# Graph network on one core: counts copied by ScalarE into a bf16 ring, four count tables fetched earlier, first eight K/V gathers issued one stage earlier

## The chip, the cores and the metric

The kernel runs on one core of one Trainium2 chip. The metric is the device time of one execution in microseconds (us), as the median of the runs. A core has TensorE (PE, matrix products, with a separate weight load PEld), VectorE (DVE), ScalarE (ACT), GpSimd (POOL) and SyncE (SP, which here only issues DMAs and waits). Each engine works through its own instructions in order; semaphores are all that ties them together. SBUF is the on-chip memory of 128 partitions, PSUM the accumulator memory that PE writes.

## What is computed

A graph has 3125 nodes with 96 features each and 103125 directed edges (50000 random pairs in both directions and one loop per node), sorted by destination. Four layers follow one another, each added to its input and layer-normalised:

```python
edge_index = jnp.stack([src, dst])
x = _layernorm(x + _L0_gnn_ref(x, L0_gnn_weight, L0_gnn_bias, src, dst))
x = _layernorm(x + _L1_gnn_ref(x, edge_index, edge_weight, W1, b1, W2, b2, W3, b3))
x = _layernorm(x + _L2_gnn_ref(x, edge_index, W1, b1, W2, b2, gn...))
x = _layernorm(x + _L3_gnn_ref(x, edge_index, edge_attr_96, Wq, bq, Wk, bk, We, be, Wv, bv))
# L0: agg = segment_sum(feat[src] * out_deg[src]**-0.5, dst) * in_deg**-0.5; agg @ W + b
# L1: three times  segment_sum((x @ W)[src] * norm, dst) + b,  norm from weighted degrees
# L2: twice        graph_norm(segment_sum((x @ W)[src], dst) + b), relu, + identity
# L3: score = exp(clip(sum(K[src] * Q[dst] * E) / sqrt(12), -5, 5)) for 8 heads;
#     segment_sum(V[src] * score, dst) / (segment_sum(score, dst) + 1e-6)
```

## The kernel before

The first three layers don't gather. They multiply by dense 3125x3125 tables: `w_blocks` (f32) holds the sum of edge weights from node s to node d, `c_blocks` (bf16) the number of such edges. Both lie in HBM as NT=25 blocks of 125 destination columns (LANES). The stages, in order:

- `examine_edges` (0 to 17 us) loads indices, checks them, and prepares per-edge numbers.
- `add_edges` (to 571 us) builds the tables. Edges lie in columns of 128. A batch g is G=8 columns (101 batches), a four q is Q4=4 columns (202 fours), a round r is four batches and moves on by about one block. For a batch DVE makes one-hot vectors: `hot_lo` (which source lane, L761), `hot_hi` (L772), `third` (L778, one part of the split edge weight), `middle` (L783, another part, for columns BY_ACT=4 to 7), and `hot` (which destination place of a window, L769, once for a four). ACT multiplies `hot_lo` by the parts of the weight (L678, twelve per batch). PE multiplies these into one PSUM bank pair per four, `ps_four[u]`, u = 0 or 1: zero (L717), counts (L723), out-degrees (L724), weights (L729). The result covers a window of REACH=20 destination columns, for 25 source tiles and two tables: 1000 elements per partition. DVE's `add` (L797) adds them to the ring `strip`, f32, [128, 2 tables, 25, 520]: four slots of 125 columns and an overlap of 20, at a column read from `ring_col`. The windows of successive fours overlap or follow on one another.
- In each round, `finish` (L803) closes a block; every fourth round `fold` (L807) adds the overlap back to the ring's beginning. ACT `convert`s the block's counts to bf16 into `counts` in five pieces of 625 elements (L668). SP stores weights (L608) and counts (L610). POOL clears the slot again with memsets (L630, L636): count head after the conversion, weight head and both tails after the store of the weights. DVE waits for `heads_clear` and `tails_clear` at the start of later rounds.
- `graph_layers` (572 to 1354 us): 150 jobs, six passes of 25 blocks. Passes 0, 4 and 5 use count tables (PE L1281), passes 1 to 3 weight tables (L1269); SP's `load(j)` fetches a job's table into a ring, four slots for counts. One count table, `first_table`, is fetched in `add_edges` already. In pass 0 the stores of the last weight block (five pieces, L1053) stand between the loads, then `wrow` (L1056) is read from HBM, and DVE's `weight_sums` (L1453) sum it in five pieces, one a job, before job 17 (`W_DEG_AT`). The stage ends with projections to K, V, Q, stored by SP to `kv_dram` (L1067) and `q3_dram` (L1072); SP waits until all have landed, and an all-engine barrier follows.
- `attention_windowed` (from 1354.6 us) walks 202 fours through a ring of ten slots: POOL gathers K/V rows (L2350, four indirect DMAs a four, indices copied by ACT L2368), SP loads edge attributes, destinations and Q rows (L2317, L2318, L2320), PE multiplies (L2441, L2443, L2455), DVE makes scores and messages (L2510 to L2530). POOL waits for `msg_ready` of the four that had its slot before.

The order on each engine is the order of the code in its block; there is no scheduler.

## Time and profile before

| | us |
|---|---|
| median of 3 runs | 2692.86 |
| lowest, highest | 2684.45, 2707.22 |
| profiled execution, device time | 2688.49 |
| its span in the profile | 2685.7 |

| engine | busy us | share of the span |
|---|---|---|
| PE | 2006.5 | 75% |
| DVE | 1384.0 | 52% |
| ACT | 1004.8 | 37% |
| POOL | 957.3 | 36% |

The profiled execution's own time is 2.8 us above its span. Shares over the whole span say little, since the stages have different limits. The page's second part divides the span in forty slices of 67 us: in slices 2 to 8 DVE shows 9 of 9 tenths, in the graph layers PE does, and in the attention none does. The rows further down are from views of single stages: windows (busy time per engine in a stretch), groups by line (mean duration of one instruction and what it waited for), waits, and the timeline (start and duration of single instructions; in it an instruction's duration overlaps the next one's by about 0.1 us, so the cost of one is read as the distance between two starts).

### The profile page before, as it was taken

The numbers are of one execution on the slowest core, as the hardware profiler recorded it, in microseconds if no ns is written. First come the engines' busy times: TensorE is split into PE (matmuls) and PEld (weight loads), VectorE is DVE, ScalarE is ACT, GpSimd is POOL, SyncE is SP. The second block draws the span as 40 slices with busy tenths as digits, with TensorE's granted clock in tenths as the row PEclk, the third lists the DMA queues.
The fourth block names the chain that finished last, engine by engine and source line by source line (L and its number), as shares of the span: only waits on it lengthen the run. The fifth ranks groups of instructions, "written<-read, shape, count | busy, mean of one in ns | idle before, by whom it ended". The sixth has DMA issues, their size and how long they took to land. (4 is left out here: it accounts for less than half of the span.)

```text
span 2685.7 us, 50009 instructions
## 1 busy us (share of the span) xinstructions
PE 2006.5 (75%) x14784; PEld 1733.1 (65%) x14785; DVE 1384.0 (52%) x3361; ACT 1004.8 (37%) x2697; POOL 957.3 (36%) x947
## 2 busy tenths in 40 slices
PE   7888888879999999999716565565656656665665
PEld 3666666657999999878515555555555555555565
DVE  6999999976111134332414444444444444444445
ACT  5788888853100011121312332333233233333332
POOL 2122223210000000000255566565655655666662
PEclk9999999989999999999755555555555555555555
DMA  1677787797888777657244444444444444444442
GB/s 49 95 122 109 116 128 117 115 197 245 308 288 292 287 288 281 215 174 243 63 129 135 127 125 125 116 132 122 124 130 121 125 118 128 129 132 124 126 134 56
DMA packets 225304, 415.59 MB, mean 155 GB/s; under 512 B 130819, under 2 KB 150297, under 8 KB 215449
## 3 DMA queue, kind: packets, MB, share of 16 engines
q1 hardware_dynamic: 186414, 334.76, 45.7%
q0 software_dynamic: 38784, 79.48, 11.4%
q8 instruction: 59, 0.97, 0.1%
q14 instruction: 47, 0.38, 0.0%
HBM read 347.71 MB, written 66.43 MB: 154 GB/s over the span
## 5 line engine op out<-in xcount | busy, mean ns | idle before, releaser
L2350 POOL DMA_INDIRECT attention_windowed_vkv<-kv_dram,ttention_windowed_vsrc x808 | 783.9, 970 | 507.9 <-issue 252.7
L2441 PE MATMUL attention_windowed_vps_e<-attention_windowed_vwe,attention_windowed_vattr 97*128 97x96 f32 x1616 | 413.1, 428 | 179.9 <-issue 113.8
L2441 PEld LDWEIGHTS attention_windowed_vps_e<-attention_windowed_vwe,attention_windowed_vattr 97*128 97x128 f32 x1616 | 370.7, 329 | 181.4 <-issue 153.5
L2455 PE MATMUL attention_windowed_vps_s<-attention_windowed_hot,attention_windowed_vmsg 128*104 128x32 f32 x1616 | 324.8, 357 | 212.3 <-issue 100.8
L2455 PEld LDWEIGHTS attention_windowed_vps_s<-attention_windowed_hot,attention_windowed_vmsg 128*104 128x104 f32 x1616 | 302.8, 286 | 253.0 <-issue 199.0
L1269 PE MATMUL graph_layers_acc<-graph_layers_w_tab,graph_layers_g 125*96 125x125 f32 x3750 | 417.7, 269 | 0.0
L1269 PEld LDWEIGHTS graph_layers_acc<-graph_layers_w_tab,graph_layers_g 125*96 125x96 f32 x3750 | 406.6, 163 | 0.0
L678 ACT ACTIVATE add_edges_hot_lo<-add_edges_hot_lo,parts 128x128 bf16<-128x128 bf16 x1212 | 372.6, 393 | 89.5 <-DVE add_edges_hot_lo L761 89.5
L2383 ACT ACTIVATE attention_windowed_vmsg<-ttention_windowed_vscore 128x32 f32<-128x32 f32 x202 | 46.5, 230 | 801.9 <-DVE ttention_windowed_vscore L2516 498.8
L729 PE MATMUL add_edges_ps_four<-add_edges_hot,add_edges_hot_lo 128*128 128x200 bf16 x2424 | 332.1, 258 | 0.0
L1099 POOL CAST graph_layers_g<-graph_layers_w_tab 125x480 bf16<-125x480 f32 x4 | 2.3, 585 | 742.5 <-ACT graph_layers_w_tab L1146 735.8
L797 DVE TENSOR_TENSOR strip<-strip,add_edges_ps_four 128x1000 f32 x202 | 244.1, 1209 | 23.3 <-PE add_edges_ps_four L729 22.5
L630 POOL MEMSET strip<- 128x500 f32 (+1 forms) x92 | 127.2, 1412 | 319.8 <-ACT add_edges_counts L668 220.9
L2443 PE MATMUL attention_windowed_vps_q<-ttention_windowed_q_rows,attention_windowed_hot_T 96*128 96x96 bf16 x808 | 119.3, 276 | 155.4 <-issue 153.0
L2530 DVE TENSOR_TENSOR ttention_windowed_sums_T<-ttention_windowed_sums_T,attention_windowed_vps_s 104x32 f32 x202 | 38.2, 189 | 365.6 <-remote 259.1
L723 PE MATMUL add_edges_ps_four<-add_edges_hot,add_edges_hot_lo 128*128 128x200 bf16 x808 | 211.8, 262 | 0.0
L2510 DVE TENSOR_TENSOR attention_windowed_vprod<-attention_windowed_vkv,attention_windowed_vps_q 128x384 f32<-128x384 f32 x202 | 110.8, 549 | 195.5 <-remote 151.1
L2443 PEld LDWEIGHTS attention_windowed_vps_q<-ttention_windowed_q_rows,attention_windowed_hot_T 96*128 96x128 bf16 x808 | 101.1, 153 | 167.1 <-issue 165.5
L1281 PE MATMUL graph_layers_acc<-graph_layers_g,graph_layers_c_tab 125*128 125x288 bf16 (+1 forms) x1400 | 196.8, 290 | 3.0 <-DMA graph_layers_c_tab<-c_blocks 2.4
L729 PEld LDWEIGHTS add_edges_ps_four<-add_edges_hot,add_edges_hot_lo 128*128 128x128 bf16 x2424 | 178.0, 99 | 1.1
L1432 DVE SCALAR_TENSOR_TENSOR graph_layers_z<-graph_layers_prod,graph_layers_dis,graph_layers_b 125x96 f32<-125x96 f32 x75 | 23.9, 318 | 298.3 <-PE graph_layers_prod L1249 298.3
L717 PE MATMUL add_edges_ps_four<-add_edges_noughts,add_edges_nought 1*128 1x500 bf16 x404 | 121.4, 380 | 64.1 <-DVE strip L797 63.7
(245 smaller groups left out, 2666.5 us busy)
## 6 DMA issues: line engine op xcount, KB each, us to landing
graph_layers_w_tab<-w_blocks SPq DMA_DIRECT2D x75, 1562.5 KB
graph_layers_c_tab<-c_blocks SPq DMA_DIRECT2D x56, 800.0 KB
attention_windowed_vattr<-in_attr_T SPq DMA_DIRECT2D x202, 192.0 KB
attention_windowed_vdrow<-dstf_dram SPq DMA_DIRECT2D x202, 192.0 KB
w_blocks<-strip SPq DMA_DIRECT2D x24, 1562.5 KB, 14.6
c_blocks<-add_edges_counts SPq DMA_DIRECT2D x24, 800.0 KB, 5.8
first_table<-c_blocks SPq DMA_DIRECT2D x19, 800.0 KB, 4.4
attention_windowed_vkv<-kv_dram,ttention_windowed_vsrc POOLq DMA_INDIRECT x808
```

Of the source, the lines that this page charges most:

```text
L630: nc.gpsimd.memset(strip[:, table, :, slot(b)][:, :, columns], 0.0).then_inc(done, 1)
L678: done = nc.scalar.activation(hot_lo[s][:, 1 + part, j, :], hot_lo[s][:, 0, j, :], ACT.Copy, scale=parts[:, part, bass.ds(g * G + j, 1)])
L717: nc.tensor.matmul(both[:, table, 0:NT * REACH], nought[:], noughts[:], start=True, stop=False)
L723: nc.tensor.matmul(cells[:, 0], hot_lo[s][:, 0, e, :], hot[s][:, e, :], start=False, stop=m == Q4 - 1)
L729: last = nc.tensor.matmul(cells[:, 1], hot_lo[s][:, 1 + part, e, :], hot[s][:, e, :], start=False, stop=m == Q4 - 1 and part == 2)
L797: nc.vector.tensor_tensor(cells, cells, ps_four[u][:, :, 0:NT * REACH].rearrange("p c (t n) -> p c t n", n=REACH), ALU.add).then_inc(added, 1)
L1269: return nc.tensor.matmul(acc[j % 2][0:D, 0:L], g[(k - 1) % 2][0:L, t, :], w_tab[s][0:L, t, :], start=t == 0, stop=t == NT - 1)
L1281: return nc.tensor.matmul(acc[j % 2][:, 0:width], c_tab[s][0:L, t, :], g3[0:L, t, 0:width], start=t == 0, stop=t == NT - 1)
L2350: nc.gpsimd.indirect_dma_start(out=kv[s][:, k, :], out_offset=None, in_=kv_dram, in_offset=bass.IndirectOffsetOnAxis(ap=src4[s][:, k:k + 1 ...
L2441: nc.tensor.matmul(ps_e[s % BANKS][:, k, :], attr[:, s, k * P:(k + 1) * P], wes[:], start=True, stop=True)
L2443: last = nc.tensor.matmul(ps_q[s % BANKS][:, k, :], hot_T[s][:, k, :], q_rows[:, s, :], start=True, stop=True)
L2455: last = nc.tensor.matmul(ps_s[s % 2], msg[s][:, k, :], hot[s][:, k, :], start=k == 0, stop=k == Q4 - 1)
```

## The change

Three edits, of which the first is the largest.

**Counts.** The ring `strip` now holds weights alone (f32, 500 elements per window), and counts have a ring of their own, `count_ring`, in bf16. A four's first column can hold counts of the four before, so DVE adds that one column (25 elements); the nineteen behind it are new, and ACT copies them out of PSUM (`copy_counts`, 475 elements, over what was there). DVE's `add` becomes an add of 25 and one of 500 elements. ACT's `convert` goes; BY_ACT falls from 4 to 3, so ACT has eleven multiplications a batch, and DVE's `middle` covers five columns (640 elements) for four. POOL converts the whole block with one copy (3125 elements per partition), folds the counts' overlap (`fold_counts`), and clears half as many elements. PE waits for `copied` and `middle_done` too; DVE and ACT wait for POOL's `ring_free`.

**Tables.** Four count tables (FIRST_TABLES) are fetched during blocks 17 to 20 of `add_edges`, and `graph_layers` starts without loads 1 to 3. The last weight block is stored in one DMA ahead of `load(4)`; `wrow` is read after `load(6)`. `weight_sums` has eight pieces and stands where DVE waits for ACT's standard deviation; `W_DEG_AT` is 18. `y5` has three buffers.

**Gathers.** POOL copies the indices of two fours (AHEAD=2) and issues their eight gathers at the end of `graph_layers`, as soon as K/V are stored. SP there waits for the Q stores only. In the attention ACT and POOL begin with four 2; SP's wait for `ones_ready` moved to PE. `examine_edges` checks in addition that no window begins 20 or more columns behind the one before (four small DVE instructions).

```diff
-                if b == NT - 3:
-                    sp.wait_ge(counts_stored, 16)
-                    sp.dma_start(first_table[:].rearrange("p t c -> p (t c)"), c_blocks[0]).then_inc(first_landed, 16)
+                q = b - (NT - 8)
+                if 0 <= q < FIRST_TABLES:
+                    sp.wait_ge(counts_stored, 16 * (q + 1))
+                    sp.dma_start(first_tables[q][:].rearrange("p t c -> p (t c)"), c_blocks[q]).then_inc(first_landed[q], 16)
...
-                clear(b, 0, head, heads_clear)
-                pool.wait_ge(weights_stored[b % SLOTS_B], 16 * (b // SLOTS_B + 1))
-                clear(b, 1, head, heads_clear)
-                clear(b, 0, tail, tails_clear)
-                clear(b, 1, tail, tails_clear)
...
+            def fold_counts(b):
+
+                pool.wait_ge(added, groups_of(b))
+                pool.wait_ge(copied, groups_of(b))
+                nc.gpsimd.tensor_tensor(count_ring[:, :, 0:REACH], count_ring[:, :, 0:REACH], count_ring[:, :, RING:RING + REACH],
+                                        ALU.add).then_inc(count_folded, 1)
+                pool.wait_ge(count_folded, b // SLOTS_B + 1)
...
+                pool.wait_ge(added, groups_of(b))
+                pool.wait_ge(copied, groups_of(b))
+                if b > 0:
+                    pool.wait_ge(counts_stored, 16 * b)
+                nc.gpsimd.tensor_copy(counts[:, :, 0:LANES], count_ring[:, :, slot(b)]).then_inc(converted, 1)
+                if first:
+                    pool.wait_ge(converted, b + 1)
+                    nc.gpsimd.memset(count_ring[:, :, 0:REACH], 0.0)
+                pool.sem_inc(ring_free, 1)
...
-                done = nc.scalar.activation(counts[:, some, 0:LANES], strip[:, 0, some, bass.ds((r + 2) % SLOTS_B * LANES, LANES)], ACT.Copy)
...
+            def copy_counts(q, at):
+
+                act.wait_ge(columns_added, q + 1)
+                cells = ps_four[at[1]][:, 0, 0:NT * REACH].rearrange("p (t n) -> p t n", n=REACH)[:, :, 1:REACH]
+                nc.scalar.activation(count_ring[:, :, 1:RING + REACH][:, :, bass.ds(at[0], REACH - 1)], cells, ACT.Copy).then_inc(copied, 1)
...
+                        if later_batch and j == 2:
+                            copy_counts(2 * g - 2, (at[0], 0))
+                        if later_batch and j == 6:
+                            copy_counts(2 * g - 1, (at[1], 1))
+                        if j == 1 and k == batches[0] and reaches(r, 3):
+                            act.wait_ge(ring_free, r - 2)
...
                             pe.wait_ge(added, q - 1)
+                            pe.wait_ge(copied, q - 1)
...
+                            if e == BY_ACT:
+                                pe.wait_ge(middle_done, g + 1)
...
-                nc.vector.tensor_tensor(cells, cells, ps_four[u][:, :, 0:NT * REACH].rearrange("p c (t n) -> p c t n", n=REACH),
-                                        ALU.add).then_inc(added, 1)
+                if reaches(q, 1):
+                    dve.wait_ge(copied, q)
+                first = count_ring[:, :, bass.ds(at, 1)]
+                nc.vector.tensor_tensor(first, first, new[:, 0, :, 0:1], ALU.add).then_inc(columns_added, 1)
+                nc.vector.tensor_tensor(cells, cells, new[:, 1], ALU.add).then_inc(added, 1)
...
                 if reaches(r, 3):
-                    dve.wait_ge(heads_clear, 2 * (r - 2))
+                    dve.wait_ge(ring_free, r - 2)
+                    dve.wait_ge(heads_clear, r - 2)
                     dve.wait_ge(overlap_clear, (r - 3) // SLOTS_B + 1)
                 if reaches(r, 4):
-                    dve.wait_ge(tails_clear, 2 * (r - 3))
+                    dve.wait_ge(tails_clear, r - 3)
...
-            load(1)
...
-            load(2)
-            load(3)
...
+            sp.dma_start(w_blocks[NT - 1].rearrange("p (t c) -> p t c", c=L), strip[:, :, 0:L]).then_inc(last_stored, 16)
+            load(4)
+            load(5)
...
-            for j in range(4, 4 + 5):
-                load(j)
-                some = chunk(j - 4)
-                sp.dma_start(w_blocks[NT - 1].rearrange("p (t c) -> p t c", c=L)[:, some, :], last_weights[:, some, :]).then_inc(last_stored, 16)
-            load(9)
-            sp.wait_ge(last_stored, 16 * 6)
+            load(6)
+            sp.wait_ge(last_stored, 16 * 2)
             sp.dma_start(wrow[:], w_blocks[:, L + 1, :].rearrange("b (t c) -> b t c", c=L)).then_inc(wrow_loaded, 16)
...
-            sp.wait_ge(tables_stored, 16 * (2 + 2 * CHUNKS))
+                sp.dma_start(q3_dram[area, :].rearrange("(t p) c -> p t c", p=L), g3[0:L, chunk(c), 0:D3]).then_inc(q3_stored, 16)
+            sp.wait_ge(q3_stored, 16 * (1 + CHUNKS))
+            pool.wait_ge(early_src_ready, AHEAD)
+            pool.wait_ge(kv_stored, 16 * (1 + CHUNKS))
+            for q in range(AHEAD):
+                for k in range(Q4):
+                    nc.gpsimd.indirect_dma_start(
+                        out=early_kv[q][:, k, :], out_offset=None, in_=kv_dram,
+                        in_offset=bass.IndirectOffsetOnAxis(ap=early_src[q][:, k:k + 1], axis=0)).then_inc(early_landed[q], 16)
...
+                if j < NT and 0 <= j - (W_DEG_AT - 2 - W_SUM_PARTS) < W_SUM_PARTS:
+                    weight_sums(j - (W_DEG_AT - 2 - W_SUM_PARTS))
                 dve.wait_ge(sd_ready, n + 1)
...
-            for s in range(SLOTS):
+            for s in range(AHEAD, SLOTS):
                 gather(0, s)
```

What stands in a row on DVE in `add_edges`, from a batch's first one-hot to its `middle`, before (after it come the second `hot` and the second four's add):

```order
L761 TENSOR_TENSOR add_edges_hot_lo<-add_edges_lane_of,add_edges_lo 128x8x126
L772 TENSOR_TENSOR add_edges_hot_hi<-add_edges_tile_of,add_edges_hi 128x208
L778 TENSOR_TENSOR add_edges_hot_lo<-add_edges_hot_lo,add_edges_third 128x1024
L769 TENSOR_TENSOR add_edges_hot<-add_edges_place_of,add_edges_place 128x800
L797 ISA
L797 TENSOR_TENSOR strip<-strip,add_edges_ps_four 128x50x20
L783 TENSOR_TENSOR add_edges_hot_lo<-add_edges_hot_lo,add_edges_middle 128x512
```

and after; an ISA row ahead of an add sets its address:

```order
L809 TENSOR_TENSOR add_edges_hot_lo<-add_edges_lane_of,add_edges_lo 128x8x126
L820 TENSOR_TENSOR add_edges_hot_hi<-add_edges_tile_of,add_edges_hi 128x208
L826 TENSOR_TENSOR add_edges_hot_lo<-add_edges_hot_lo,add_edges_third 128x1024
L817 TENSOR_TENSOR add_edges_hot<-add_edges_place_of,add_edges_place 128x800
L849 ISA
L849 TENSOR_TENSOR count_ring<-count_ring,add_edges_ps_four 128x25
L850 ISA
L850 TENSOR_TENSOR strip<-strip,add_edges_ps_four 128x25x20
L831 TENSOR_TENSOR add_edges_hot_lo<-add_edges_hot_lo,add_edges_middle 128x640
```

Each 1000-element add has become one of 25 and one of 500, and `middle` (L783, now L831) has grown.

ACT in a batch of `add_edges`, after the change; `parts` are the multiplications, L703 is the first of the copies of counts (L701 and the ISA row set its address):

```order
L714 ACTIVATE add_edges_hot_lo<-add_edges_hot_lo,parts 128x128
L714 ISA
L714 ACTIVATE add_edges_hot_lo<-add_edges_hot_lo,parts 128x128
L701 REGISTER_ALU
L703 ISA
L703 ACTIVATE count_ring<-add_edges_ps_four 128x25x19
L714 ISA
L714 ACTIVATE add_edges_hot_lo<-add_edges_hot_lo,parts 128x128
```

Two such copies stand among the multiplications of a batch, after the 6th and the 10th of the eleven. Before, two copies of 625 elements from `strip` to `counts` stood in most batches.

POOL for the first blocks, before (`x2`: twice in a row):

```order
L636 MEMSET strip 128x50x20
L630 MEMSET strip 128x25x20 x2
L630 MEMSET strip 128x25x105 x2
L630 MEMSET strip 128x25x20 x2
L630 MEMSET strip 128x25x105 x2
```

and after, for a block that folds and the next:

```order
L648 TENSOR_TENSOR count_ring<-count_ring 128x25x20
L656 MEMSET count_ring 128x25x20
L662 COPY add_edges_counts<-count_ring 128x25x125
L665 MEMSET count_ring 128x25x20
L670 MEMSET strip 128x25x20
L672 MEMSET strip 128x25x20
L673 MEMSET strip 128x25x105
L662 COPY add_edges_counts<-count_ring 128x25x125
L672 MEMSET strip 128x25x20
L673 MEMSET strip 128x25x105
```

Of POOL's operations before, all in this stretch write only; now one copy a block, and a two-input add every fourth, read SBUF.

## Rows read from the trace of the kernel before

**Rows 1.** windows; columns: stretch, length, busy us (count) per engine, PE clock, DMA

```profile
150.00:250.00 100.00, 87.25 (x858) 62.76 (x857) 99.87 (x162) 83.38 (x255) 29.17 (x22) 1.00 0.73 112
```

**Rows 2.** timeline, DVE, one batch; start us, duration us, line, operation

```profile
281.51 0.70 DVE L761 TENSOR_TENSOR add_edges_hot_lo<-add_edges_lane_of,add_edges_lo 128x1008 bf16<-128x1008 bf16 x1
...
282.99 0.59 DVE L769 TENSOR_TENSOR add_edges_hot<-add_edges_place_of,add_edges_place 128x800 bf16<-128x800 bf16 x1
283.48 1.21 DVE L797 TENSOR_TENSOR strip<-strip,add_edges_ps_four 128x1000 f32 x1
284.58 0.44 DVE L783 TENSOR_TENSOR add_edges_hot_lo<-add_edges_hot_lo,add_edges_middle 128x512 bf16<-128x512 bf16 x1
284.92 0.59 DVE L769 TENSOR_TENSOR add_edges_hot<-add_edges_place_of,add_edges_place 128x800 bf16<-128x800 bf16 x1
...
286.51 0.70 DVE L761 TENSOR_TENSOR add_edges_hot_lo<-add_edges_lane_of,add_edges_lo 128x1008 bf16<-128x1008 bf16 x1
```

**Rows 3.** groups, 100 to 550 us, DVE; count, busy us, mean ns

```profile
L797 DVE TENSOR_TENSOR strip<-strip,add_edges_ps_four 128x1000 f32 x176 | 212.9, 1210 | 0.8 <-PE add_edges_ps_four L729 0.2
```

**Rows 4.** waits, 100 to 550 us; total us, times, longest us

```profile
PE add_edges_ps_four L717 <- DVE strip L797: 56.8, 87, 1.4
...
DVE strip L797 <- PE add_edges_ps_four L729: 0.2, 1, 0.2
```

**Rows 5.** groups, 100 to 550 us, ACT

```profile
L678 ACT ACTIVATE add_edges_hot_lo<-add_edges_hot_lo,parts 128x128 bf16<-128x128 bf16 x1054 | 324.5, 393 | 55.6 <-DVE add_edges_hot_lo L761 55.6
L668 ACT ACTIVATE add_edges_counts<-strip 128x625 bf16 x110 | 79.0, 718 | 11.5 <-DVE strip L803 11.5
```

**Rows 6.** timeline, ACT, a copy out of PSUM

```profile
1304.46 0.57 ACT L1151 COPY graph_layers_w_tab<-graph_layers_acc 96x500 f32<-96x500 f32 x1 [1.36 <-PE graph_layers_prod L1329]
```

**Rows 7.** groups, 100 to 550 us, POOL

```profile
L630 POOL MEMSET strip<- 128x2625 f32 x44 | 99.8, 2297 | 0.0
L630 POOL MEMSET strip<- 128x500 f32 x44 | 23.3, 529 | 305.5 <-ACT add_edges_counts L668 213.2 <-DMA w_blocks<-strip 92.3
```

**Rows 8.** timeline, POOL, its only conversion of 128 partitions

```profile
569.26 0.99 POOL L644 CAST add_edges_hot_lo<-strip 128x625 bf16<-128x625 f32 x1 [14.57 <-DVE strip L803]
```

**Rows 9.** timeline, POOL, two operations that read SBUF

```profile
1311.94 1.07 POOL L1101 TENSOR_TENSOR graph_layers_rest<-graph_layers_w_tab,graph_layers_g 125x480 f32<-125x480 f32 x1
1313.07 0.59 POOL L1103 CAST graph_layers_g<-graph_layers_rest 125x480 bf16<-125x480 f32 x1
```

**Rows 10.** timeline, DVE, at the same moment

```profile
1311.88 0.16 DVE L1522 TENSOR_TENSOR graph_layers_var<-graph_layers_st 125x5 f32<-125x5 f32 x1
1312.11 0.92 DVE L1524 TENSOR_TENSOR graph_layers_dif<-graph_layers_dif 125x5 f32<-125x5 f32 x1
```

**Rows 11.** page, DMA issues: count, KB each, us from issue to landing

```profile
w_blocks<-strip SPq DMA_DIRECT2D x24, 1562.5 KB, 14.6
```

**Rows 12.** windows of pass 0, with and without weight sums; columns as rows 1

```profile
624.90:652.00 27.10, 24.83 (x196) 18.90 (x195) 20.20 (x74) 7.19 (x28) 0.00 (x0) 1.00 0.61 207
652.00:678.10 26.10, 25.39 (x207) 20.26 (x206) 16.00 (x78) 13.01 (x50) 0.00 (x0) 1.00 0.79 299
```

**Rows 13.** timeline, PE, the stall in pass 0

```profile
620.45 2.34 PE L1281 MATMUL graph_layers_acc<-graph_layers_g,graph_layers_c_tab 125*128 125x289 bf16 x12 [2.35 <-DMA graph_layers_c_tab<-c_blocks]
```

**Rows 14.** timeline, DVE, one weight sum

```profile
632.03 1.31 DVE L1453 TENSOR_REDUCE graph_layers_wsum<-graph_layers_wrow 25x25 f32<-25x625 f32 x1
```

**Rows 15.** timeline, end of graph_layers and start of attention

```profile
1340.82 0.87 SPq L1067 DMA_DIRECT2D kv_dram<-graph_layers_w_tab  x1
...
1355.80 1.16 POOL L2350 DMA_INDIRECT attention_windowed_vkv<-kv_dram,ttention_windowed_vsrc  x1 [0.99 <-ACT ttention_windowed_vsrc L2368]
1357.27 0.96 POOL L2350 DMA_INDIRECT attention_windowed_vkv<-kv_dram,ttention_windowed_vsrc  x1 [0.30 <-issue]
...
1359.18 0.33 SPq L2317 DMA_DIRECT2D attention_windowed_vattr<-in_attr_T  x1
```

**Rows 16.** timeline, POOL, its first wait in attention

```profile
1416.09 0.95 POOL L2350 DMA_INDIRECT attention_windowed_vkv<-kv_dram,ttention_windowed_vsrc  x1 [9.76 <-DVE attention_windowed_vmsg L2520]
```

210 lines of the change are left out of this document (123 added, 87 removed).

## Prediction

> **What bounds the kernel now.** I read the windows of the stages first. From 50 to 568 us `add_edges` runs, and in a window of 100 us DVE is busy 99.87, PE 87, ACT 83, POOL 29 [rows 1]: DVE sets that stage's pace. The waits confirm it: DVE's add waited for PE once in 450 us, for 0.2 us, while PE waited for DVE's adds 56.8 us in all [rows 4]. So PE would need about (450 - 56.8) / 88 batches = 4.47 us a batch where DVE needs 5.00, the distance between two `hot_lo` starts [rows 2]. In the graph layers PE sets the pace; the rows show where it does not: a stall of 2.35 us for a count table [rows 13], and a window with weight sums in which 196 matmuls of the count product took 27.1 us where the next window did 206 in 26.1 [rows 12]. In the attention no engine is full; its first POOL wait for a free slot comes at 1406 to 1416 us [rows 16].
>
> **Part 1, DVE in add_edges.** An add of 1000 elements costs 1.10 us from start to start [rows 2] (176 of the 202 stand in one group with this mean duration, [rows 3]). One of 500 costs 0.55 if all of it scales, about 0.58 with a fixed part; one of 25 about 0.1, since even a five-element operation shows 0.16 with its overlap [rows 10]. Saved: 1.10 - 0.68 = 0.42 an add, 0.84 a batch. `middle` grows by 128 elements: 800 elements cost 0.49 and 512 cost 0.34 [rows 2], so +0.07. Net 0.77 a batch, times 101 batches = -78 us; six folds at half size, -3 us.
>
> Whether the others can follow: ACT made twelve multiplications and 1.25 conversions a batch; now eleven at 0.29 (393 ns less the overlap of 0.10, [rows 5]) = 3.2, and two copies out of PSUM at 0.46 (a 500-element one took 0.57 with overlap, [rows 6]) = 0.9, so 4.1 of DVE's new 5.00 - 0.77 = 4.23. PE needs the 4.47 above, more than 4.23: at most, since a little of it is the wait for ACT. Without another cost, a round of four batches would therefore be PE's 17.9 us, and not DVE's 17.2.
>
> **Part 2, POOL now reads SBUF.** Its memsets before only write. The 3125-element copy of a block does not appear in this trace. Bounds: a memset's slope, (2297 - 529) / 2125 = 0.83 ns an element [rows 7], gives 2.7 us; a conversion of 480 elements took 0.59 us [rows 9], 1.22 ns an element, 3.8 us, or 3.2 if 0.11 of it is fixed as in the memsets; the one conversion on 128 partitions took 0.99 us for 625, beside two casts of DVE [rows 8], 4.9 us. I take 2.9, nearest to the slope and the conversion with its fixed part taken off, because the new copy reads 2-byte elements in rows of 125.
>
> POOL has the time for it (29 of 100 us busy). What matters is DVE: at 1311.94 POOL ran a two-input operation of 1.07 us, to 1313.01; a DVE operation of two SBUF inputs on five elements, started 1312.11, took 0.92 us and ended at 1313.03, where the same kind took 0.16 just before, at a moment with no such POOL operation beside it [rows 9, 10]. So a POOL operation that reads SBUF holds up a DVE operation with two SBUF inputs until it ends. Nearly all of DVE's work in a batch is that; only the adds, which take one input from PSUM, probably run beside it. (The Trainium skill, "SBUF — State Buffer", section "Who interferes with whom", says the same: two SBUF inputs on DVE contend with a GpSimd operation that reads SBUF, not with one that only writes, and the other engine blocks fully. The trace agrees, 0.92 us against 0.16. By that rule this change trades DVE work for DVE standstill.) I count 2.5 us a copy, since POOL most likely gets in beside an add of 0.6 us half of the time or more: 24 copies x 2.5 = +60 us. `fold_counts` (500 elements, two inputs, 1.07 for 480, [rows 9]) seven times, less an overlap: +5. PE and ACT catch up during the standstill: a lag of 4 x (4.47 - 4.23) = 1.0 us a round fits into 2.5.
>
> (The Trainium skill, "GPSIMD Engine Reference", section 3, has a read-bound body at 1.03 cycles an element: 3125 x 1.03 / 1.2 GHz = 2.7 us, an estimate from that page alone; with it the sum would be 5 us lower. The memset slope gives the same.)
>
> Accumulation: -78 - 3 + 60 + 5 = -16 us. The round goes from 4 x 5.00 + 0.5 = 20.5 to about 19.8. The store of the weights (14.6 us, [rows 11]) and the 0.53 us memset behind it still end about 3.5 us ahead of the next use. Copy at 2.7 gives -21; at 3.8 (3.4 net), +5; at 4.9 (4.5 net), +32.
>
> **Part 3, tables and weight sums.** The stall of 2.35 goes, because `wrow` and the five pieces no longer stand between the loads [rows 13]. Behind it PE ran 12 matmuls in 2.34 where it usually takes 1.66: another 1.3 us over that job until the pace returned. Weight sums of 1.31 us [rows 14] sat in DVE's loop: 196 matmuls at the next window's pace are 24.8 us, so 2.3 was lost in 27.1 [rows 12]. Moved to where DVE waits 0.4 to 0.5 us for ACT, in eight pieces of 0.8 us, they still cost some. Together about -6 us; bounds 0 (the large loads collide with the undivided store) and -8. The third `y5` buffer is worth nothing: DVE's and ACT's split of each chunk sets that pace, and POOL was ahead.
>
> **Part 4, early gathers.** The last K/V store is issued at 1340.82 and, with 0.6 MB in 768-byte pieces, I take it as landed at about 1350; attention's first gather starts at 1355.80, the second 1.47 later, and the rest 1.26 apart [rows 15]. Eight early ones from 1350.3 end at 1360.4. POOL holds the barrier about 7 us longer than SP's Q stores did, so attention starts near 1361.5; SP's loads move from 1359.18 to about 1362, but POOL's ninth gather from 1366.1 (1357.27 + 7 x 1.26) to 1362.6. The stage starts later by 2.5 for PE and earlier by 3.5 for POOL. POOL runs on until its slots are full [rows 16], and the DVE fours there are far apart while gathers run; I take -3, between +7 (the barrier's delay carried to the end) and -10. `examine_edges` gets four small DVE operations at 0.15: +0.6.
>
> **Sum.** +0.6 - 16 - 6 - 3 = -24 us. On the profiled execution's 2688.5 that is 2664; its time is 4 us under the median of the runs shown, which spread over 23 us. I say 2665, 1.0% under the median.
>
> **Rivals.**
> - *Copies don't stop DVE* (POOL's read is slow only in itself, or DVE's one-hots pass). Against it: rows 9 and 10. Then PE sets 4.47 x 4 + 0.3 = 18.2 a round: 25 rounds x -2.3 = -57 in the accumulation, total -65: 2627. Chance 0.12.
> - *The copy costs 3.8 us*: conversion rate without a fixed part, or DVE and POOL slow each other. Accumulation +5, total about -4: 2686, no change. Chance for this and for gathers without gain, 0.31.
> - *Slower*: the copy at the rate of [rows 8], 4.9 us. DVE stands 4.5 us of every round, 24 times, +32 in accumulation, total +24: 2714. It turns the sign from about 4.0 us a copy on. For it: this is the only row with 128 partitions. Against it: that row had DVE casts beside it. Chance 0.10.
> - *The barrier*: POOL's eight gathers delay everything 7 us and POOL, which fills its slots anyway, gains nothing: +10 against my sum, 2675, within 1%. In the 0.31 above in part.
>
> **How the numbers follow.** My case (copy 2.7 to 3.2, blocking) 0.47: 2650 to 2680. No blocking 0.12, same 0.31, slower 0.10. A measurement of this kernel tells about 1%, 27 us, from no change, so faster means under 2666. Half or more of my own case lies there with the no-blocking one and a part where the attention falls lucky: faster 0.46, same 0.43, slower 0.11. The range 2628 to 2700 leaves 2 in 10 out.
>
> **What would show it.** In the profile after: one-hots on DVE of 0.4 to 0.7 us that last 2 to 3 us once a round, each ending with POOL's copy; the copy's duration, 2.9 us; adds of 500 at 0.68; distance between weight stores about 19.8 us (18.2 if nothing blocks, over 21 if the copy is at the upper bound). In pass 0 no PE wait for `c_tab`. At 1340 to 1361 us, eight gathers and the barrier behind them. The forecast is wrong if POOL's copy takes over 3.5 us, if DVE waits for `copied` or PE for `middle_done`, or if the attention's length shifts by more than 10 us.

## The result, and the profile after

The change made the kernel slower. Four runs gave 2723.6 to 2790.5 us, median 2761.2, against 2689.1 for the kernel before in the same session; the ratio is 1.0205, interval 1.0148 to 1.0262. The run of 2790.5 us was in a slower state and is left out of the ratio, which goes by the other three. The forecast was 2665, range 2628 to 2700. The profiled execution took 2759.6 us, its span is 2757.5, 71.8 more than the span before. This table divides both spans at the same instructions (the last c_blocks store of `add_edges`, PE's first matmul with a weight table, SP's last K/V store, SP's first load of the attention):

| stage | before, us | after, us | difference |
|---|---|---|---|
| to the end of the tables | 570.8 | 638.8 | +68.0 |
| pass 0, with the barrier ahead of it | 107.3 | 101.0 | -6.3 |
| passes 1 to 5 and projections | 662.7 | 660.5 | -2.2 |
| last K/V store to the attention's start | 13.8 | 25.8 | +12.0 |
| attention | 1331.1 | 1331.5 | +0.4 |

So nearly all of the loss lies in the accumulation, where the forecast had -16. Two windows of it after the change (length, busy us and count of PE, PEld, DVE, ACT, POOL, then the granted TensorE clock, DMA share, GB/s); the window before is [rows 1]:

```profile
150.00:250.00 100.00, 89.56 (x665) 60.12 (x663) 76.21 (x152) 64.59 (x192) 24.99 (x16) 0.74 0.57 88
350.00:450.00 100.00, 85.38 (x770) 60.43 (x768) 89.98 (x180) 74.78 (x226) 27.99 (x17) 0.90 0.71 107
```

DVE has fallen from 99.87 to 76.21 busy, so it is no longer what sets the pace, and PE's clock from 1.00 to 0.74 of its 2.4 GHz. PE multiplied 665 times in 100 us where it did 858 before, and was busy 90 us all the same. The groups of DVE and POOL in 100 to 550 us (busy us, mean ns, idle time before and its releaser) answer to [rows 3, 7]:

```profile
L850 DVE TENSOR_TENSOR strip<-strip,add_edges_ps_four 128x500 f32 x150 | 100.4, 669 | 0.4 <-issue 0.4
L826 DVE TENSOR_TENSOR add_edges_hot_lo<-add_edges_hot_lo,add_edges_third 128x1024 bf16<-128x1024 bf16 x75 | 90.2, 1202 | 0.0
...
L849 DVE TENSOR_TENSOR count_ring<-count_ring,add_edges_ps_four 128x25 f32 x150 | 39.2, 261 | 66.2 <-issue 51.8 <-PE add_edges_ps_four L777 12.4 <-ACT count_ring L703 0.2
L831 DVE TENSOR_TENSOR add_edges_hot_lo<-add_edges_hot_lo,add_edges_middle 128x640 bf16<-128x640 bf16 x75 | 36.2, 483 | 0.0
```

```profile
L662 POOL COPY add_edges_counts<-count_ring 128x3125 bf16<-128x3125 bf16 x19 | 54.2, 2852 | 83.3 <-DVE strip L855 83.3
```

POOL's copy takes 2852 ns (forecast 2.9 us), the 500-element add 669 ns, 0.58 from start to start. `third` (L826) had 705 ns before and has 1202 as a mean, because 15 of the 75 met a copy and took 3.3 us; the others took 0.68. The waits of the same stretch (total us, times, longest us), against [rows 4]:

```profile
PE add_edges_ps_four L763 <- ACT count_ring L703: 53.3, 35, 2.8
DVE count_ring L849 <- issue: 51.8, 39, 2.6
...
DVE count_ring L849 <- PE add_edges_ps_four L777: 12.4, 16, 2.5
```

Before, DVE waited 0.2 us for PE here in all. Now it stands 51.8 + 12.4 us before its column add; the profile puts the larger part down to "issue". The single waits show PE as the releaser: each of the 31 that lasted over 1 us ended 0.19 us after PE's last matmul for that four, while ACT's copy had been done for 1.4 us or more, and each lies in a stretch of low clock or within 3 us of its end. One round in the timeline shows how it comes about, POOL first, then DVE, then PE:

```profile
218.32 2.87 POOL L662 COPY add_edges_counts<-count_ring 128x3125 bf16<-128x3125 bf16 x1 [5.39 <-DVE strip L855]
```

```profile
218.46 3.27 DVE L826 TENSOR_TENSOR add_edges_hot_lo<-add_edges_hot_lo,add_edges_third 128x1024 bf16<-128x1024 bf16 x1
...
229.88 0.27 DVE L849 TENSOR_TENSOR count_ring<-count_ring,add_edges_ps_four 128x25 f32 x1 [1.84 <-PE add_edges_ps_four L777]
```

```profile
223.24 0.58 PE L763 MATMUL add_edges_ps_four<-add_edges_noughts,add_edges_nought 1*128 1x500 bf16 x2 [2.40 <-ACT count_ring L703]
...
225.79 1.01 PE L763 MATMUL add_edges_ps_four<-add_edges_noughts,add_edges_nought 1*128 1x500 bf16 x2
```

`third` starts 0.14 us behind POOL's copy and ends 0.5 us after it: it lasts 3.27 us instead of 0.68. All 24 copies did the same to the one-hot that they met: it lasted 2.2 to 3.3 us and ended 0.4 to 0.6 us after the copy. Until DVE comes to its next column add, ACT has nothing to copy and PE no free PSUM bank: PE stands 2.40 us. Less than 2 us after it has begun again, its clock falls. The windows of 2 us around it:

```profile
222.00:224.00 2.00, 0.76 (x6) 0.38 (x7) 2.00 (x7) 1.47 (x5) 0.00 (x0) 1.00 1.27 127
224.00:226.00 2.00, 2.00 (x21) 1.57 (x18) 2.00 (x5) 1.39 (x5) 0.00 (x0) 0.73 1.25 128
226.00:228.00 2.00, 2.00 (x12) 1.16 (x11) 2.00 (x5) 2.00 (x8) 0.00 (x0) 0.50 1.22 135
240.00:242.00 2.00, 2.00 (x11) 0.96 (x8) 0.77 (x3) 1.25 (x5) 0.00 (x0) 0.50 0.00 0
242.00:244.00 2.00, 2.00 (x22) 1.67 (x22) 1.21 (x3) 1.65 (x5) 0.00 (x0) 1.00 0.00 0
```

From about 225 to 242 us PE works at 1.2 GHz: its two zero matmuls take 1.01 us instead of 0.58 (the two PE rows above), a four 3.8 us instead of 2.1. Now DVE waits for PE, at 229.88 for 1.84 us and so on, until the clock is back. The distance between two weight stores, one a round, was 27.8 us in this round and 29.5 in the next; in rounds where the clock fell for 3 us or not at all it was 18 to 22, 25 with a fold (86.1 for the four rounds from 382.14 on, 21.5 each, against 20.5 before). From 60 to 560 us PE had 19 gaps of 2 us or more, and there were 14 falls of the clock; in windows of 1 us each fall shows 2 to 4 us after the beginning of a gap of 2.06 us or longer. Time at low clock added up to 157 us. Before, there was no gap over 1.4 us, and 14 us at low clock, behind two gaps of 1.38 us.

### The profile page after: what moved, and what is told of

Its sections match the earlier page's. It is cut to its first block and busy times, and to the rows that moved or that the text cites. A ratio compares the mean times of both kernels' runs of the same rounds, so it can differ in the third digit from the quotient of the medians.

```text
span 2757.5 us, 50923 instructions
## 1 busy us (share of the span) xinstructions
PE 2055.8 (75%) x14784; PEld 1761.1 (64%) x14785; DVE 1377.0 (50%) x3570; ACT 1005.3 (36%) x2677; POOL 955.6 (35%) x948
## 5 line engine op out<-in xcount | busy, mean ns | idle before, releaser
L2419 POOL DMA_INDIRECT attention_windowed_vkv<-kv_dram,ttention_windowed_vsrc x600 | 573.5, 956 | 402.0 <-DVE attention_windowed_vmsg L2590 217.4
L777 PE MATMUL add_edges_ps_four<-add_edges_hot,add_edges_hot_lo 128*128 128x200 bf16 x2424 | 375.8, 280 | 0.0
L714 ACT ACTIVATE add_edges_hot_lo<-add_edges_hot_lo,parts 128x128 bf16<-128x128 bf16 x1111 | 353.7, 389 | 49.5 <-DVE add_edges_hot_lo L809 46.5
L1345 PE MATMUL graph_layers_acc<-graph_layers_g,first_table 125*128 125x288 bf16 (+1 forms) x1875 | 259.2, 289 | 14.7 <-DVE graph_layers_g L1435 12.5
L2419 POOL DMA_INDIRECT early_kv<-kv_dram,early_src x200 | 191.6, 958 | 125.3 <-DVE attention_windowed_vmsg L2590 66.5
L771 PE MATMUL add_edges_ps_four<-add_edges_hot,add_edges_hot_lo 128*128 128x200 bf16 x808 | 229.7, 284 | 0.0
L1345 PEld LDWEIGHTS graph_layers_acc<-graph_layers_g,first_table 125*128 125x128 bf16 x1875 | 184.0, 99 | 63.1 <-issue 11.6
L777 PEld LDWEIGHTS add_edges_ps_four<-add_edges_hot,add_edges_hot_lo 128*128 128x128 bf16 x2424 | 195.8, 107 | 7.4
L763 PE MATMUL add_edges_ps_four<-add_edges_noughts,add_edges_nought 1*128 1x500 bf16 x404 | 135.2, 418 | 69.3 <-ACT count_ring L703 68.4
L703 ACT ACTIVATE count_ring<-add_edges_ps_four 128x475 f32 x202 | 116.0, 574 | 124.1 <-DVE count_ring L849 123.4
```

Source lines behind the costliest of these rows:

```text
L703: nc.scalar.activation(count_ring[:, :, 1:RING + REACH][:, :, bass.ds(at[0], REACH - 1)], cells, ACT.Copy).then_inc(copied, 1)
L714: done = nc.scalar.activation(hot_lo[s][:, 1 + part, j, :], hot_lo[s][:, 0, j, :], ACT.Copy, scale=parts[:, part, bass.ds(g * G + j, 1)])
L763: nc.tensor.matmul(both[:, table, 0:NT * REACH], nought[:], noughts[:], start=True, stop=False)
L771: nc.tensor.matmul(cells[:, 0], hot_lo[s][:, 0, e, :], hot[s][:, e, :], start=False, stop=m == Q4 - 1)
L777: last = nc.tensor.matmul(cells[:, 1], hot_lo[s][:, 1 + part, e, :], hot[s][:, e, :], start=False, stop=m == Q4 - 1 and part == 2)
L1345: return nc.tensor.matmul(acc[j % 2][:, 0:width], c_tab[s][0:L, t, :], g3[0:L, t, 0:width], start=t == 0, stop=t == NT - 1)
```

## The experiments

The theory after this reading: POOL's read stops DVE, that lets PE run dry, its clock falls, and at low clock PE sets the pace. The first rival: the new, longer loop (DVE adds a column, ACT copies, PE may start, DVE adds) is what makes PE late, with or without POOL.

### POOL's copy replaced by a write

```diff
-nc.gpsimd.tensor_copy(counts[:, :, 0:LANES], count_ring[:, :, slot(b)]).then_inc(converted, 1)
+nc.gpsimd.memset(counts[:, :, 0:LANES], 0.0).then_inc(converted, 1)
```

> The changed kernel with POOL's copy of a block's counts replaced by a memset of the same 3125 bf16 elements, about as long (2.7 us), which writes SBUF and reads nothing. The conversion is left out, so the count tables are zeros. Theory (POOL's read stops DVE, PE then runs dry for 2.4 us and its granted clock falls to 0.5 for 10 to 17 us): no one-hot over 1 us on DVE, granted clock 0.97 or more from 150 to 450 us, a round at PE's pace of about 18.2 us, accumulation 524 - 57 = 467 us instead of 592, total about 2760 - 125 = 2635 us. Rival (the longer loop DVE's column add, ACT's copy, PE, DVE's add makes PE late and lowers the clock, with or without POOL): accumulation stays above 560 us, clock about 0.8, total above 2730 us.

Measured (`e1`): 2662.4 us, ratio to the kernel before 0.9889 (0.9853 to 0.9925). Tables done at 539.4 us. Window and group, columns as above:

```profile
150.00:250.00 100.00, 90.85 (x903) 65.95 (x900) 92.85 (x213) 86.34 (x266) 32.97 (x23) 1.00 0.75 119
```

```profile
L826 DVE TENSOR_TENSOR add_edges_hot_lo<-add_edges_hot_lo,add_edges_third 128x1024 bf16<-128x1024 bf16 x42 | 28.7, 684 | 0.0
...
L849 DVE TENSOR_TENSOR count_ring<-count_ring,add_edges_ps_four 128x25 f32 x82 | 21.5, 262 | 10.1 <-ACT count_ring L703 5.0 <-PE add_edges_ps_four L777 3.4 <-issue 0.9
```

```profile
L662 POOL MEMSET add_edges_counts<- 128x3125 bf16 x11 | 29.7, 2704 | 19.0 <-DVE strip L855 19.0
```

The memset is as long as the copy (2704 against 2852 ns) and stands in the same place; `third` is back at 684 ns, the clock at 1.00. A POOL operation that only writes held no one-hot up, one that reads costs 99 us of the tables' time (638.8 - 539.4). The rival falls as the cause of the loss. But the gain is 31 us and not 57: the weight stores are 76.5 us apart for four rounds, 19.1 a round, where I had 18.2. Six stops are left in this kernel: `fold_counts` reads SBUF too, and the DVE operation that it meets loses 0.9 us (`hot_hi` 1.24 us for 0.37), 5.3 us over the stage. A round needs some 0.25 us a batch over the 4.47 that I took for PE, and no engine is full: DVE has 7% idle (the waits of L849), PE 9%, ACT 14%. That the loop over DVE, ACT and PE is what costs it is argued from these waits, not shown; the last experiment below tries to shorten that loop and wins nothing.

### The same read put into the kernel before

```diff
+pool.wait_ge(block_done, b + 1)
+nc.gpsimd.tensor_copy(spare[:], parts[:].rearrange("p a e -> p (a e)").bitcast(BF16)[:, 0:2500])
 pool.wait_ge(converted, b + 1)
 clear(b, 0, head, heads_clear)
```

> The kernel before, with one more POOL operation a block: a copy of 2500 bf16 elements from a table that nobody writes to a spare tile, for which nobody waits. Theory: once a round a one-hot of DVE lasts about 2.3 us more (2500 x 0.92 ns), PE stands 2 us, and its granted clock falls to 0.5 in some rounds. Stops alone: 24 x 2.3 less what lies beside adds = +35 to +50 us; with falls of the clock, in a DVE-bound stage where PE at 1.2 GHz needs about 7.6 us a batch, +60 to +110: total 2750 to 2800 us. Rival (chain length, not POOL's read): this kernel has the old chain, so clock 0.98 to 1.00 as before and total within +50 us at most, 2690 if the read does not stop DVE.

Measured (`e2`): 2736.2 us, 1.0161 (1.0121 to 1.0200). Tables done at 610.1, 39 us later than before. The copy nobody waits for and the one-hot beside it:

```profile
281.31 2.35 POOL L639 COPY add_edges_spare<-parts 128x2500 bf16<-128x2500 bf16 x1 [3.72 <-DVE strip L806]
```

```profile
281.44 2.75 DVE L781 TENSOR_TENSOR add_edges_hot_lo<-add_edges_hot_lo,add_edges_third 128x1024 bf16<-128x1024 bf16 x1
```

2.75 us instead of 0.70, for a POOL operation of 2.35. There is no new chain here, and still PE gaps of 1.7 to 2.05 us arise and 72 us at low clock. The total is a little under what I expected (2750 to 2800): DVE's batch of 5.0 us leaves PE more time at either clock. The 39 us account for most of the 42 us; the attention, which the edit does not touch, was 13 us longer in this execution, and pass 0 was 4.5 us shorter.

### Five pieces beside the adds

```diff
-nc.gpsimd.tensor_copy(counts[:, :, 0:LANES], count_ring[:, :, slot(b)]).then_inc(converted, 1)
+for n in range(5):
+    pool.wait_ge(columns_added, min(groups_of(b) + n + 1, NQ))
+    some = slice(n * NT // 5, (n + 1) * NT // 5)
+    done = nc.gpsimd.tensor_copy(counts[:, some, 0:LANES], count_ring[:, some, slot(b)])
+done.then_inc(converted, 1)
```

> The changed kernel with POOL's copy in five pieces of 625 elements (0.65 us each), each started when DVE has added the column of one further four, that is while DVE's 500-element add (one SBUF input, 0.58 us) runs. Nothing is left out. Theory: each piece lies beside the add and holds the next one-hot up by 0 to 0.3 us; no PE gap over 1 us, granted clock 0.95 or more, round 18.2 to 18.8 us, accumulation about 475 to 490 us, total 2645 to 2660 us. Rival (total time under POOL's reads counts, in one piece or five, or the chain sets the pace): the accumulation stays above 540 us and the total above 2700.

Measured (`e3`): 2678.3 us, 0.9947 (0.9926 to 0.9969), tables done at 561.6. This is faster than both kernels, by 0.5% of the one before. One piece on POOL, and DVE beside it:

```profile
298.55 0.71 POOL L665 COPY add_edges_counts<-count_ring 128x625 bf16<-128x625 bf16 x1 [5.33 <-DVE count_ring L853]
```

```profile
298.24 0.67 DVE L854 TENSOR_TENSOR strip<-strip,add_edges_ps_four 128x500 f32 x1
298.82 0.78 DVE L835 TENSOR_TENSOR add_edges_hot_lo<-add_edges_hot_lo,add_edges_middle 128x640 bf16<-128x640 bf16 x1
```

The add of 500 elements (one SBUF input, one from PSUM) runs its usual 0.67 us with the piece beside it, and `middle` behind it loses 0.3 us (0.78 for 0.48). Longest PE gap 1.4 us, 14 us at low clock. The sign and the mechanism are as expected, the size is not: a round takes 20.0 us (79.9 to 80.2 between the stores of four rounds), not 18.2 to 18.8, since to the 19.1 of the memset kernel come five losses of 0.2 to 0.3.

### Five pieces elsewhere

The same five pieces with no waits between them (`e5`), and with each started after the four's whole add (`e11`):

```diff
-    pool.wait_ge(columns_added, min(groups_of(b) + n + 1, NQ))
+    pool.wait_ge(added, min(groups_of(b) + n + 1, NQ))
```

> The changed kernel with POOL's copy in five pieces of 625 elements one after the other, with no wait between them. Theory (what hurts is one stop of 2.7 us, which lets PE run dry): DVE's operations get in between the pieces, so no single one lasts over 1.4 us, but DVE's sum of lost time in a round is the same, 5 x 0.6 = 3 us, and falls in the same 5 us: PE still waits 2 to 2.5 us once a round and its clock falls as often as in the changed kernel: total 2740 to 2770. Rival (only an uninterrupted stop lowers the clock): PE's gap breaks into parts under 1.3 us, clock 0.97 or more, total 2700 to 2710 (21.2 us a round, against 20.5 before, less 8 elsewhere).

> As e3_pieces (early gathers included), but each of the five pieces starts when DVE has finished a four's whole add, so that it meets a one-hot instead of the add. Theory: a piece then stops DVE for its whole 0.65 us, five times a round, spread over five fours: 0.4 us more a piece than in e3_pieces, 2 us more a round, less what DVE waited for PE or ACT anyway: +25 to +45 us on e3_pieces, total 2703 to 2723; PE's gaps stay under 1.6 us, granted clock mostly 0.95 or more. Rival (only the length of one stop matters, not its place): within 8 us of e3_pieces, 2678.

Measured: back to back 2733.9 us, 1.0132 (1.0100 to 1.0163), between theory and rival: 5 gaps of 2 us or more, 28 of 0.8 to 2, nine falls, 116 us at low clock. Its one-hots last up to 1.20 us (`third`, 0.68 undisturbed) and 1.07 (`hot`, 0.57) beside a piece. Breaking the stop up shortens most gaps and takes away part of the falls, not all. Behind the adds: 2738.7 us, 1.0177 (1.0157 to 1.0197), well above the 2703 to 2723 expected. My expectation left the clock out: 12 falls behind gaps of 1.5 to 2.3 us, 102 us at low clock. POOL's piece and DVE's one-hot also slow each other there:

```profile
373.59 0.81 POOL L665 COPY add_edges_counts<-count_ring 128x625 bf16<-128x625 bf16 x1 [3.81 <-DVE strip L854]
375.63 1.10 POOL L665 COPY add_edges_counts<-count_ring 128x625 bf16<-128x625 bf16 x1 [1.23 <-DVE strip L854]
```

```profile
373.75 1.07 DVE L821 TENSOR_TENSOR add_edges_hot<-add_edges_place_of,add_edges_place 128x800 bf16<-128x800 bf16 x1
```

0.81 and 1.10 us for a piece that takes 0.71 beside an add. Between `e3` and `e11` lies only when a piece starts, and so which DVE operation it meets: 60 us, a part of it through the clock (14 us at low clock against 102).

### Filling PE's gap

If the gap is what lowers the clock, more work for PE at that place should make the changed kernel faster.

```diff
 at = spots(g)
+if k == 1:
+    for _ in range(9):
+        nc.tensor.matmul(ps_fill[:, 0:NT * REACH], nought[:], noughts[:], start=True, stop=True)
```

and in the second version

```diff
+    for _ in range(25):
+        nc.tensor.matmul(ps_fill[:, 0:PLACES], place_of[:, 0:P], place_of[:], start=True, stop=True)
```

> The changed kernel with work added: nine matmuls of zeros (one row, 500 columns, a spare PSUM bank; about 2.4 us at full clock) on PE ahead of the second batch of each round, where PE stands waiting for ACT's copy while POOL's copy holds DVE. DVE is stopped as long as in the changed kernel. Theory (the gap on PE lowers its granted clock, and the low clock makes PE the late one): gap under 0.5 us, clock 0.97 or more, each round at what an undisturbed one of the changed kernel takes, 21.2 us: accumulation about 535 to 545 us instead of 592, total 2700 to 2712, faster with more work. Rival (the clock falls for another reason, and DVE's stop itself is the cost): clock 0.8 as in the changed kernel, accumulation 592 or more, total 2760 or more.

> As e6_fill, but the matmuls that fill PE's gap are 25 of the size of the stage's own (128 rows, 128 x 200, bf16, about 2.3 us) instead of nine of one row. In e6_fill the long gaps were gone (1 of 2 us or more, against 19) and the time at low clock had halved (80 us against 157), not gone. Theory (the clock follows how much PE multiplies, and one-row matmuls count for little): low-clock time from 60 to 560 us under 30 us, accumulation 535 to 550 us after the first round, total 2700 to 2715 us. Rival (not the gap but something else about this kernel lowers the clock): 80 us or more at low clock, total 2740 or more.

Measured: with one-row matmuls (`e6`) 2741.1 us, 1.0168 (1.0119 to 1.0216), tables at 621.1, 80 us at low clock; neither theory nor rival. With full ones (`e10`) 2709.5 us, 1.0064 (1.0046 to 1.0081), as the theory had it: tables at 591.3, 27 us at low clock, 47 us earlier than the changed kernel, with 2.3 us more PE work a round:

```profile
250.00:350.00 100.00, 94.61 (x953) 70.98 (x950) 96.81 (x197) 79.97 (x245) 31.14 (x22) 1.00 0.67 106
```

```profile
321.52 2.31 PE L758 MATMUL add_edges_ps_fill<-add_edges_place_of 128*128 128x200 bf16 x25 [0.63 <-issue]
```

```profile
318.60 3.29 DVE L830 TENSOR_TENSOR add_edges_hot_lo<-add_edges_hot_lo,add_edges_third 128x1024 bf16<-128x1024 bf16 x1
```

DVE is stopped as before (3.29 us for `third`), the filler lies in the time where PE waited, and the clock holds. So the stop costs 591.3 - 539.4 = 52 us against the memset kernel, and the clock another 638.8 - 591.3 = 47. The split is not exact: 27 us at low clock are left here against 11 in the memset kernel's accumulation, so that 52 is rather too much for the stop alone and 47 rather too little for the clock.

### The conversion given back to ACT

POOL's copy goes, ACT makes five copies of 625 elements a round from `count_ring` as it did from `strip`:

```diff
+if u in CONVERT_AT and reaches(r, 2):
+    convert(r, CONVERT_AT.index(u))
```

> The changed kernel with the conversion given back to ACT (five pieces of 625 elements a round at 0.62 us, as before the change, out of the bf16 ring), so POOL reads SBUF only in the fold every fourth round. Nothing is left out. Theory (POOL's read is the harm, the rest of the counts edit is sound): no long one-hot, granted clock 0.97 or more; ACT has 16.4 + 3.1 = 19.5 us a round and sets the pace: accumulation about 490 to 505 us, total 2660 to 2680. Rival (the columns on DVE and the copies on ACT are no gain in themselves): accumulation 524 us or more, total 2690 or more.

Measured (`e8`): 2703.7 us, 1.0031 (1.0016 to 1.0046), tables at 588.0. Missed: I expected 2660 to 2680. These are the numbers of the rival. ACT is busy 93 us in 100 and a round takes 21.1 to 21.7 us (84.2 to 86.6 between stores four rounds apart), more than the 20.5 before the change:

```profile
250.00:350.00 100.00, 85.51 (x797) 60.58 (x797) 83.87 (x193) 93.05 (x264) 15.18 (x15) 0.93 0.70 114
```

```profile
PE add_edges_ps_four L774 <- ACT count_ring L698: 26.2, 24, 1.9
DVE count_ring L860 <- ACT count_ring L698: 23.0, 17, 2.0
```

DVE waits 23 us in 200 for ACT's copies. The conversions stand in ACT's queue ahead of copies that PE and DVE wait for, so they probably delay the loop and not ACT's sum alone (not tried apart); the clock was low for 44 us besides. With POOL's copy in pieces (`e3`) the same columns on DVE and copies on ACT were a gain of 9 us in the stage; with the conversion on ACT they were a loss of 17.

### The early gathers

> The changed kernel with AHEAD = 0: no gathers in the layers' stage, ACT and POOL begin the attention with four 0; SP still waits only for the Q stores there, POOL for the K/V stores. Theory: from the issue of the last K/V store to the attention's start about 14 to 16 us instead of 25.8, the attention itself 1331 us as in both kernels, so about 10 us less than the changed kernel (2750), the accumulation unchanged at 560 to 600 us. Rival (early gathers are worth something in the attention that its later start hides): the attention grows by 8 us or more and the total stays the same.

> Five pieces beside DVE's adds (as e3_pieces), and no early gathers (AHEAD = 0). Theory (the early gathers delay the attention's start by 10 to 11 us and give back about 6 in it): 3 to 6 us under e3_pieces, total 2672 to 2676. Rival (they are worth their delay): 2678 or more.

> As e3_pieces with AHEAD = 1: four early gathers, 5 us, in place of eight. The Q stores let SP go about 15.5 us after the last K/V store is issued; four gathers from 12.6 us end at 17.6. Theory: tail 19 to 21 us (25.5 with eight, 16 with none), attention 1332 to 1340, total 2670 to 2680: no difference that can be measured to either neighbour. Rival (the gain in the attention comes with the first four): 2668 or less.

```diff
-AHEAD = 2
+AHEAD = 0
-            pool.wait_ge(early_src_ready, AHEAD)
```

This on the changed kernel (`e4`), on the kernel with five pieces (`e7`), and `AHEAD = 1` on the latter, with its wait kept (`e9`). Measured: the changed kernel without early gathers 2760.6 us, 1.0252 (1.0193 to 1.0311), where 2750 was expected; five pieces without them 2676.4, 0.9932 (0.9912 to 0.9953), against 2678.3 with them, in another session (3 to 6 us less were expected: the runs can't tell theory from rival); five pieces with one four ahead 2700.5, 1.0033 (1.0014 to 1.0052), a miss. The tail and the attention in the profiled executions:

| early fours | last K/V store to the attention's start, us | attention, us |
|---|---|---|
| 0, new code (e4, e7, e12 below) | 15.4, 16.8, 16.5 | 1337.2, 1348.1, 1351.9 |
| 0, old code (before, e2) | 13.8, 18.3 | 1331.1, 1343.8 |
| 1 (e9) | 20.0 | 1354.4 |
| 2 (after, e1, e3, e5, e6, e8, e10, e11) | 23.0 to 25.8 | 1325.6 to 1338.6, mean 1331.5 |

The delay repeats in every execution: with eight gathers the new code needs 6 to 10 us more than without. The attention's length changes by 13 us and more between executions of the same code, and the one of `e7` was the longest of its eight (2692.5 us against a median of 2676.4). By the means of these few executions the attention was 14 us shorter with eight gathers than without in the new code (6 by the two executions of the old), so they may pay for their delay or not; `e9`'s 1354.4 stays unexplained. In the two pairs of medians (2761.2 and 2760.6, 2678.3 and 2676.4) the early gathers are worth nothing that can be measured.

### A copy placed earlier

```diff
-if later_batch and j == 6:
+if later_batch and j == 5:
```

> As e7_pieces_no_early (2676), with ACT's second copy of counts one column earlier in the batch (after column 5 instead of column 6), since DVE's waits for ACT's copy (9 us in 200) and PE's (19 us in 200) are what is left in the stage. Theory (the loop DVE's column add, ACT's copy, PE, DVE's add has no slack): ACT reaches that copy 0.3 us earlier and PE starts the next four up to 0.3 us earlier: 0.1 to 0.3 us a batch, total 2650 to 2668. Rival (ACT then waits for DVE's column add, and nothing is won): 2674 to 2682.

Measured (`e12`): 2690.3 us, 0.9983 (0.9965 to 1.0001). Tables at 561.7 against 563.3 us: nothing won in the stage that it changes. The rival's mechanism shows in the waits from 150 to 350 us: ACT waited 7.3 us for DVE's column add, against 4.2 in `e7`, and DVE and PE waited for ACT's copy as long as there (9.9 and 20.4 us against 9.1 and 19.6). The total lies above what theory and rival had, and its interval above that of `e7` (0.9912 to 0.9953); the edit's own stage doesn't account for these 14 us, and their cause is open.

## Why the prediction was wrong

**What held.** DVE set the pace before. The copy took 2.85 us (forecast 2.9) and does stop a DVE operation with two SBUF inputs, which the trace before had shown on one five-element operation and which the memset and the read in the old kernel prove. The rule of the Trainium skill ("SBUF — State Buffer", section "Who interferes with whom"), that a DVE instruction with two SBUF inputs contends with a GpSimd instruction that reads SBUF and not with one that only writes it, agrees: 3.27 us beside the copy, 0.68 beside the memset. The 500-element add cost 0.58. Pass 0 gained 6.3 us where 6 were forecast; over all executions with the new code it took 99.0 to 101.0 us, with the old one 107.3 and 102.8. But its stall did not go, as "no PE wait for `c_tab`" had it. It was shorter:

```profile
666.26 1.66 PE L1345 MATMUL graph_layers_acc<-graph_layers_g,first_table 125*128 125x289 bf16 x12 [1.43 <-DMA first_table<-c_blocks]
```

This is 1.43 us for 2.35, and the old code in `e2` had 1.35. So a part of the 6.3 is scatter, and that the number came out is partly luck.

**The step that failed.** "PE and ACT catch up during the standstill: a lag of 4 x (4.47 - 4.23) = 1.0 us a round fits into 2.5." They caught up a part only (24 stops of 2.6 us, 62 in all, cost 52, see below), and then they ran dry. This step is also what let the sum take DVE's whole saving, 78 us, in a stage where PE by its own figure could follow for 0.53 of the 0.77 us a batch. With two PSUM bank pairs PE can be at most two fours ahead of DVE; it had finished them at 220.84, 0.35 us before the copy ended, and stood 2.4 us. I had taken it that PE is not the bound from a window in which its clock was 1.00 [rows 1], and never asked what the clock does when PE stands still for that long. No rival held a mechanism for it: the slower one was a longer copy. None of the signs of a wrong forecast covered it either: the wait that appeared, PE's for ACT's copy (53.3 us), is not among them. The row at [rows 12, 13] had a hint, which I used as a term of 1.3 us and not as a warning: behind a stall of 2.35 us, PE needed 2.34 us for what usually takes 1.66. The same trace shows why (window, then as above; the last three numbers are granted clock, DMA share, GB/s):

```profile
620.00:621.00 1.00, 0.55 (x5) 0.47 (x6) 0.00 (x0) 0.00 (x0) 0.00 (x0) 1.00 1.06 352
622.00:623.00 1.00, 1.00 (x6) 0.66 (x5) 0.00 (x0) 0.00 (x0) 0.00 (x0) 0.50 0.88 349
```

The granted clock had fallen to 0.50 behind the stall, 3.2 us after its beginning. The kernel before already held the mechanism.

**The account of the accumulation.** Forecast -16 us, measured +68, 84 more. The forecast was -81 (DVE's saving and the folds at half size) and +65 (24 stops and `fold_counts`). The memset kernel gives the first term: without the copy's stops -31, and -36 without the 5 us of the six `fold_counts` too, instead of -81, and of the -57 of my first rival. A batch needed about 4.7 us and not 4.23 or 4.47; the loop over DVE, ACT and PE is the likely reason. The second: the copy's stops cost 52 us where I had 60, the folds 5 as forecast, so that this term was about right. The third, the clock, 47 us in the profiled execution, had no term. So of the 84 us some 45 lie in a saving that did not come, 47 in the clock, and 8 go off because the stops hid a part of the lag. (-31, 52 and 47 add up to 68 by construction: they are differences along four measured times, 570.8, 539.4, 591.3 and 638.8.)

Which of the 24 gaps are followed by a fall differs between executions: the kernel without early gathers has the same accumulation, and from 60 to 560 us it had 13 falls and 130 us at low clock for 14 and 157, at other rounds; its tables were done at 641.2 us. This may be why the three runs of the changed kernel that the ratio goes by spread over 39 us (mean granted clock 0.721 in the fastest, 0.715 in the two others); only one of them was traced.

**Part 3 and 4.** The early gathers started 12.6 us behind the last K/V store's issue and not 9.5, the stage's barrier moved by 12 us and not 7, and the attention took as long as before. Forecast for both -3, measured +12.4 in this execution. The rival "the barrier" had the mechanism (delay without gain), but 7 us for it: +10 against the sum of -3. The chain, in the changed kernel's own timeline:

```profile
1400.29 3.72 SPq L1120 DMA_DIRECT2D kv_dram<-graph_layers_w_tab  x1
...
1412.87 1.17 POOL L1167 DMA_INDIRECT early_kv<-kv_dram,early_src  x1 [14.21 <-DMA kv_dram<-graph_layers_w_tab]
...
1421.85 0.95 POOL L1167 DMA_INDIRECT early_kv<-kv_dram,early_src  x1 [0.30 <-issue]
1426.04 0.24 SPq L2378 DMA_DIRECT2D attention_windowed_vwe<-in_we  x1
```

## What to carry to other kernels

Before moving work to an idle engine, ask what that work reads: on this chip a copy on POOL that reads SBUF stopped the busiest engine for its whole length, a memset of the same length did not, and in pieces beside operations with a PSUM input it cost 0.2 to 0.3 us a piece. Then follow the stop to the engines behind it and ask whether TensorE will stand still for a microsecond or two: after such a gap it ran at half its clock here, more often than not, and become the bound that it was not. Here a sum of savings on DVE said little, since PE stood 6% above it (4.47 against 4.23 us a batch): 36 us of 81 came.

## What the runs showed of the hardware

- The granted clock fell from 2.4 to 1.2 GHz 2 to 4 us after the beginning of PE gaps of 1.4 us and more, in the kernel before too (two gaps of 1.38 us), and stayed there for 3 to 20 us (once 24, in `e4`). Not every gap is followed by a fall: 14 of the 19 over 2 us in the changed kernel, 6 of the 14 of 1.4 to 1.9 us in `e8`.
- Nine matmuls of one row in the gap (2.05 us) left 80 us at low clock, and ten of the twelve falls there had no gap of 0.9 us in the 5 us ahead of them; 25 matmuls of 128 rows (2.31 us) left 27 us. For the clock the two are not the same, though PE counts as busy in both.
- POOL's piece of 625 elements takes 0.71 us beside DVE's add and up to 1.10 against a one-hot, which itself grows from 0.57 to 1.07: either engine can be the one that waits.
